# Two attentions on one core: row maxima of four heads in one quad, division by block transposes, interleaved tiles

## The chip, the cores and the metric

One core of a Trainium2 chip runs the whole kernel. The metric is device time in microseconds (us), the median of some runs. The core's engines each work through their own list of instructions in order and meet by semaphores: TensorE (PE in the profile, its weight loads PEld), VectorE (DVE), ScalarE (ACT), GpSimd (POOL), and SyncE (SP), which here only issues DMAs.

## The reference, cut to what matters

A block of two transformer layers over 2048 tokens of width 256. The change touches the two attentions of the second layer, a1 (tokens on themselves, 2048 keys) and a2 (tokens on a context of 1601 keys), both with 16 heads of width 32:

```
q = einsum('bsc,hcd->bhsd', xn, wq); k = einsum('btc,hcd->bhtd', yn, wk); v = einsum('btc,hcd->bhtd', yn, wv)
a = softmax(einsum('bhsd,bhtd->bhst', q, k) * D ** (-0.5), axis=-1)
if causal:
    mask = (arange(t)[None, :] > arange(s)[:, None]).astype(a.dtype)
    a = a * mask
o = einsum('bhst,bhtd->bhsd', a, v)
```

In a1 the mask comes after the softmax and keeps the keys *behind* the query (t > s). So the divisor of a query is a sum over all keys, while the values are summed over the later keys only.

## The kernel before, in words

`attention_stacked` runs once for a1 and once for a2. Four heads form a group (128 = 4 x 32 partitions), and 512 queries a chunk, so there are 4 groups x 4 chunks = 16 chunks, counted by n; n // 4 is the group, n % 4 the chunk in it. Keys go in tiles of 128: 16 in a1, 13 in a2 (the last has 65 rows). A step m is one key tile of one chunk.

*Units ahead of the loop.* q and k are projected in fp32, split by DVE into an f16 high part and an f16 rest (L1240, L1242), and copied by 12 DMAs a unit (L1123) so that 96 partitions hold high, rest and high of one head: one f16 matmul over 96 rows gives a score of nearly fp32 accuracy. `before` lists this lead-in for chunk 0; v units (four key tiles each) stand in it ahead of the first maxima.

*Row maxima.* Every score has to be lowered by its query's maximum before the exponential. For that TensorE computes all scores of chunk n + 1 during chunk n once more (L1338), 512 keys (401 in a2) of one head and 128 queries at a time, into one of three PSUM tiles wb, and DVE reads each with a maximum (L1266): 64 such units a chunk. At its end the 16 x 128 maxima are transposed (L1357), negated on DVE (L1296) and copied by four DMAs into row 96 of qs, so that the score matmul (97 rows) subtracts them.

*A step.* Four score matmuls (L1372, L1369 for passed tiles) go into three PSUM tiles sc in turn; ACT takes the exponential of each into a ring e of weight tiles (3 in a1, 4 in a2). One step later TensorE adds the tile's values into po (L1395, four heads abreast in four column strips) and its weights, against ones, into pd (L1416). Some tiles' weights POOL adds up instead (L1177), and TensorE takes POOL's sum at the chunk's end (L1413). In a1 a tile on the diagonal is first multiplied by a triangle on POOL (L1166). A *passed* tile, one whose keys lie before every query of the chunk, counts in the divisor only: queries go on the partitions and ACT's own sum along the row gives the divisor (L1215). Chunk 0, 1, 2 and 3 of a group have 0, 4, 8 and 12 passed tiles of 16, and all of them come first. `work_at` spreads the units of chunk n + 1 (maxima, projections, division) over the steps, between the matmuls.

*Division.* At a chunk's end ACT copies po and pd out (L1187, L1189). TensorE brings the divisors to 128 x 16 (L1345), DVE adds the passed part and takes reciprocals (L1274, L1276, L1279), TensorE transposes them (L1348), DVE copies (L1282), TensorE spreads them over 128 x 512 (L1354), and DVE multiplies (L1286). After the last chunk the divisions of the last two chunks follow each other.

The order of the work is written out: each engine walks its list, and the places are fixed by `before`, `during`, `work_at` and the loop over m in the code of TensorE.

## Time and profile before

| | |
|---|---|
| median of 3 runs | 3877.21 us (3872.72 to 3889.8) |
| span of the profiled execution, which is its own time | 3882.5 us |
| mean granted clock of TensorE | 0.917 of 2.4 GHz |
| busy in the whole span | PE 87%, DVE 64%, ACT 50%, POOL 37% |
| lead-in and loop of a1 | 70.7 and 918.3 us |
| loop of a2 | 804.4 us |

The page gives no other time for the profiled execution than its span. A share over the whole span mixes stages with other limits; each stage has to be read by itself. A row of a timeline gives start, duration, engine, line, operation, destination <- sources, count, and in brackets the idle time before with what ended it.

### The profile page before, as it was taken

What the parts mean: (1) busy time and instruction counts of PE and PEld (TensorE: products, weight loads), DVE (VectorE), ACT (ScalarE), POOL (GpSimd) and SP (SyncE); (2) the same over time, 40 slices, a digit from 0 to 9 for tenths busy, and PEclk for the clock granted to TensorE, in tenths of its full rate; (3) what the DMA queues carried; (4) which work ended last, traced back from release to release, by engine and by line L of the source; (5) the groups of instructions that cost most, each with busy time, mean ns of one, the idle gap of its engine ahead of it and who ended that gap; (6) DMA issues with size and microseconds to landing.
All of it is one profiled execution on the core that took longest, in us unless ns stands there. A gap on an engine that the chain in (4) does not pass through costs nothing. (4 is left out here: it accounts for less than half of the span.)

```text
span 3882.5 us, 65515 instructions
## 1 busy us (share of the span) xinstructions
PE 3392.2 (87%) x22711; PEld 1574.6 (41%) x22711; DVE 2480.8 (64%) x4757; ACT 1950.3 (50%) x3913; POOL 1423.1 (37%) x719
## 2 busy tenths in 40 slices
PE   5999999725994899999999986899999998969998
PEld 2333333414773233333332264233333232657776
DVE  5877687374114778777787355777777772555665
ACT  2777777421112257566666733255555555423443
POOL 2000000253222241434226140366666666505553
PEclk7999899866997799999999887799999999969999
DMA  1000000177772100100000030100000000437445
GB/s 58 11 15 10 13 6 6 66 271 257 229 241 91 33 13 9 25 6 17 17 9 5 1 107 23 39 14 17 14 15 14 8 9 1 130 112 258 93 83 116
DMA packets 163212, 239.02 MB, mean 62 GB/s; under 512 B 35859, under 2 KB 132826, under 8 KB 155994
## 3 DMA queue, kind: packets, MB, share of 16 engines
q1 hardware_dynamic: 142698, 209.40, 16.9%
q0 software_dynamic: 19056, 24.88, 3.5%
q8 instruction: 176, 2.88, 0.3%
q14 instruction: 130, 1.06, 0.1%
q10 hardware_dynamic: 1152, 0.79, 0.1%
HBM read 136.44 MB, written 68.92 MB: 53 GB/s over the span
## 5 line engine op out<-in xcount | busy, mean ns | idle before, releaser
L1266 DVE TENSOR_REDUCE a_part_max<-a_wb 128x1 f32<-128x512 f32 (+1 forms) x2048 | 1162.0, 625 | 232.3 <-PE a_wb L1338 221.7
L1218 ACT ACTIVATE a_e<-a_sc 128x512 f32<-128x512 f32 (+1 forms) x1472 | 795.2, 599 | 693.2 <-PE a_sc L1372 686.3
L1177 POOL TENSOR_TENSOR a_part_sum<-a_part_sum,a_e 128x2048 f32<-128x2048 f32 x160 | 724.6, 4528 | 103.3 <-ACT a_e L1218 87.1
L1338 PE MATMUL a_wb<-a_ks,a_qs 96*128 96x512 f16 (+1 forms) x2048 | 738.9, 372 | 26.5 <-DVEq L1246 9.5
L1372 PE MATMUL a_sc<-a_qs,a_ks 97*128 97x512 f16 (+1 forms) x1472 | 545.7, 384 | 11.7 <-DMA a_qs<-a_neg_max 8.1
L757 DVE TENSOR_REDUCE xa_part_max<-xa_mx 128x2 f32<-128x802 f32 x512 | 471.4, 986 | 128.1 <-PE xa_mx L864 125.4
L693 ACT ACTIVATE xa_e<-xa_sc 128x512 f32<-128x512 f32 (+1 forms) x832 | 445.6, 597 | 130.2 <-PE xa_sc L851 122.7
L1338 PEld LDWEIGHTS a_wb<-a_ks,a_qs 96*128 96x128 f16 x2048 | 200.6, 98 | 620.6 <-DVE a_part_max L1266 451.6
L1395 PE MATMUL a_po<-a_e,a_v 128*32 128x512 f32 (+1 forms) x2432 | 324.0, 605 | 1.9 <-ACT a_dc L1189 1.0
L1166 POOL TENSOR_TENSOR a_em<-a_e,a_later 128x512 f32<-128x512 f32 x64 | 80.9, 1265 | 579.1 <-issue 365.8
L887 PE MATMUL xa_po<-xa_e,xa_v 128*32 128x256 f32 (+1 forms) x3328 | 269.5, 396 | 7.5 <-ACT xa_oc L743 2.6
L1215 ACT ACTIVATE a_e<-a_sc 128x512 f32<-128x512 f32 x384 | 223.4, 646 | 29.4 <-PE a_sc L1369 28.5
L1372 PEld LDWEIGHTS a_sc<-a_qs,a_ks 97*128 97x128 f16 (+1 forms) x1472 | 145.5, 100 | 175.3 <-ACT a_e L1218 65.2
L864 PE MATMUL xa_mx<-xa_khi,xa_qhi 32*128 32x401 f16 x1024 | 180.1, 351 | 19.7 <-DVE xa_part_max L757 15.3
L1416 PE MATMUL a_pd<-a_e,ones 128*32 128x512 f32 (+1 forms) x1440 | 193.0, 608 | 0.0
L2607 POOL DMA_INDIRECT routed_sums<-moe_ye,moe_ids x79 | 140.1, 1773 | 141.2 <-DVE moe_ye L2750 136.7
L851 PE MATMUL xa_sc<-xa_qs,xa_ks 49*128 49x512 f16 (+1 forms) x832 | 176.7, 393 | 12.6 <-DMA xa_qs<-xa_neg_max 12.6
L2646 PE MATMUL moe_g<-wall,moe_xt 128*128 (+1 forms) x666 | 171.5, 315 | 1.0 <-ACT moe_xt L2698 0.8
L2646 PE MATMUL moe_up<-wall,moe_xt 128*128 (+1 forms) x666 | 169.8, 314 | 0.0
L635 POOL CAST xa_qhi<-xa_raw 128x512 f16<-128x512 f32 x16 | 9.8, 610 | 429.4 <-ACT xa_raw L705 421.7
L1369 PE MATMUL a_sc<-a_ks,a_qs 97*128 97x512 f16 x384 | 149.1, 407 | 8.8 <-ACT a_e L1215 7.1
L1175 POOL COPY a_part_sum<-a_e 128x2048 f32<-128x2048 f32 x28 | 52.9, 1890 | 278.2 <-ACT a_e L1218 270.7
(362 smaller groups left out, 4589.5 us busy)
## 6 DMA issues: line engine op xcount, KB each, us to landing
experts_w_up<-in_we SPq DMA_DIRECT2D x32, 1024.0 KB, 6.5
wall<-expert_halves SPq DMA_DIRECT2D x18, 1088.0 KB, 7.1
experts_w_down<-in_we SPq DMA_DIRECT2D x32, 512.0 KB, 6.0
a_qs<-a_stage SPq DMA_DIRECT2D x360, 32.0 KB, 1.9
moe_xr<-sorted_rows SPq DMA_DIRECT2D x79, 136.5 KB, 2.1
a_ks<-a_stage SPq DMA_DIRECT2D x336, 32.0 KB, 1.9
choose_whole<-in_wm SPq DMA_DIRECT2D x18, 544.0 KB, 9.0
expert_halves<-choose_cut SPq DMA_DIRECT2D x18, 544.0 KB, 8.3
```

The source lines that it names most:

```text
L693: act.activation(e[:r, m % ering, j, :], src[:r, :], ACT.Exp, scale=scale).then_inc(s_taken, 1)
L757: dve.tensor_reduce(part_max[:, 2 * h:2 * h + 2, t, c], src[:, :, :mxw], AX.X, ALU.max).then_inc(m_taken, 1)
L887: last = pe.matmul(po[h:h + SLOT, q], w, e[:r, m % ering, j, q], start=(kt == first and part == 0), stop=stop)
L1177: pool.tensor_tensor(part_sum[:, :, :], part_sum[:, :, :], tile, ALU.add).then_inc(pool_added, 1)
L1215: act.activation(e[:, m % ering, j, :], sc[(HG * m + j) % NSC][:, :], ACT.Exp, scale=scale, accum_out=span_sum[:, n % 2, t, j, c:c + 1]).t ...
L1218: act.activation(e[:r, m % ering, j, :], sc[(HG * m + j) % NSC][:r, :], ACT.Exp, scale=scale).then_inc(exp_done, 1)
L1266: dve.tensor_reduce(part_max[:, j, t, k:k + 1], src[:, :mxw], AX.X, ALU.max).then_inc(unit_taken, 1)
L1338: last = pe.matmul(dst[:, :mxw], qs[:STACK, j, n % NQ, P * t:P * t + P], ks[:STACK, g % 2, j, mxs[k]:mxs[k] + mxw], start=True, stop=True)
L1372: pe.matmul(sc[i % NSC][:r, :], ks[:STACK + 1, n // NCH % 2, j, P * kt:P * kt + r], qs[:STACK + 1, j, n % NQ, :], start=True, stop=True).t ...
L1395: last = pe.matmul(po[h:h + SLOT, :], w, e[:r, m % ering, j, :], start=(kt == first), stop=stop)
L1416: last = pe.matmul(pd[h:h + SLOT, :], ones[:r, :SLOT], e[:r, m % ering, j, :], start=(kt == first), stop=(kt == nkt - 1))
L2646: last = pe.matmul(dst[:, :], xt[j % 2][:, px, k, :], weights(u, pw, off + EI * k, EI), start=(k == 0 and px == 0 and pw == 0), stop=(k == ...
```

## The change

`attention_stacked` is replaced by `attention_quad`, for both attentions.

- Maxima come from the high halves alone (32 rows). The copies are laid out so that the high part of head j lies on partitions 32j, so the four heads' matmuls stand in four row strips of TensorE: a *quad* is four matmuls (128 queries, 512 keys, four heads) into one tile mx of four PSUM banks, and DVE reads it with two maxima of 2 x 512. There are 16 quads a chunk in a1 and 13 in a2 (the last is of 65 keys). mx is not doubled: the first two heads of a quad wait for DVE's first read of the quad before, the other two for its second.
- Projections, scores, transposition of the maxima and the carried divisors share two PSUM tiles sc (scores alone had three). ACT copies k and q to `raw` (one tile) and POOL splits them; ACT copies v and negates the maxima.
- Division: ACT copies po to ot and pd to dc; DVE transposes dc in blocks of 32 x 32, adds the carried divisors of the passed tiles, takes reciprocals, transposes them back, spread over a block, and multiplies. The passed part reaches the right partitions by a small matmul (carry). TensorE's three steps are gone.
- Passed and kept tiles alternate in the order of the steps. POOL adds other tiles: every other one (5 of 13 in a2 where it had 8). Values of a tile that POOL adds go in two halves of 256 columns.
- In the lead-in the v units stand behind the quads of the second span; POOL fills blanks and ones once all splits of the lead-in are done.

```diff
-def attention_stacked(nc, a, name, wqs, wks, wvs, extra, xq, nkq, xk, nkk, nkeys, scale, causal, ot, ones, bq=None, bk=None, bv=None, ering=4, ones_at=None):
+def attention_quad(nc, a, name, wqs, wks, wvs, extra, xq, nkq, xk, nkk, nkeys, scale, causal, ot, ones, ering=4):
...
-    NWB = 3 if ones_at is None else 4
-    NSC = 3
-    LEAD = 2
...
+    NST, NQ, NR, NSC = 3, 3, 1, 2
+    LEAD = 4
+    home = [(0, 1, 2), (1, 0, 2), (2, 0, 1), (3, 1, 2)]
+    bias_row = [STACK, STACK, STACK, 0]
...
-    def maxima(n, spans=range(nmx)):
-        return [("max", n, t, j, i) for i in spans for t in range(TPC) for j in range(HG)]
...
-        return own_sum and 0 < i and kt < nkt - 2 and (i >= TPC and i % 4 != 3 if causal else kt % 4 != 0)
+        if not causal:
+            return kt % 2 == 1
+        return i >= TPC and i % 4 != 3 if n % NCH == 0 else i % 2 == 1
...
+        tiles += sorted(((n, kt) for kt in range(nkt)),
+                        key=lambda x: (2 * x[1] + 1) * kept if x[1] < skipped else (2 * (x[1] - skipped) + 2) * skipped)
+    def quads(n, spans=range(nspan)):
+        return [("max", n, i) for i in range(nquad) if min(i // TPC, nspan - 1) in spans]
...
+    order = [("k", 0, 0), ("q", 0), ("k", 0, 1)]
+    for c in range(nspan):
+        order += quads(0, [c]) + ([("k", 0, c + 2)] if c + 2 < nspan else [])
+        if c == 1:
+            order += [("v", 0, b) for b in range(nvb)] + [("q", 1)]
+    order += [("rowmax", 0), ("turn", 0)]
...
+        parts = 1 if weighed or not kept or diagonal_of(last_n, last_k) is not None else 2
+        maxima = wide.get(m, [])
+        order += scores[:2] + maxima[:1]
+        order += [("pv", last_n, last_k, 0, parts)] if kept else []
+        order += scores[2:] + lone.get(m, [])
+        order += [("pv", last_n, last_k, 1, parts)] if parts == 2 else []
+        order += [("sum", last_n, last_k)] if weighed else []
+        order += maxima[1:]
+        if maxima and maxima[-1][2] == nquad - 1:
+            order.append(("rowmax", maxima[-1][1]))
...
-        wb = [ps(f"wb{i}", [P, CH]) for i in range(NWB)]
+        mx = ps("mx", [P, HG, CH])
...
+                    pool.tensor_copy(stage[:, i % NST, 0, :w], raw[:, i % NR, :w]).then_inc(high_ready, 1)
+                    pool.wait_ge(high_ready, i + 1)
+                    pool.tensor_tensor(stage[:, i % NST, 1, :w], raw[:, i % NR, :w], stage[:, i % NST, 0, :w],
+                                       ALU.subtract).then_inc(split_ready, 1)
...
+                    act.activation(raw[:, i % NR, :w], src[:, :w], ACT.Copy).then_inc(s_taken, 1)
...
-                    dve.tensor_reduce(part_max[:, j, t, k:k + 1], src[:, :mxw], AX.X, ALU.max).then_inc(unit_taken, 1)
...
+                    dve.wait_ge(m_ready, quad_at[u] + 1)
+                    for h in range(0, HG, 2):
+                        if i < TPC * nfull:
+                            dst, src = part_max[:, h:h + 2, i % TPC, i // TPC], mx[:, h:h + 2, :]
+                        else:
+                            dst = part_max[:, h:h + 2, :, nfull]
+                            src = mx[:, h:h + 2, :TPC * tail].rearrange("p j (t k) -> p j t k", t=TPC)
+                        dve.tensor_reduce(dst, src, AX.X, ALU.max).then_inc(m_taken, 1)
...
+                    dve.transpose(tr[:, :], dc[:, :]).then_inc(norm_step, 1)
+                    dve.reciprocal(inverse[:, :], den).then_inc(norm_step, 1)
+                    dve.transpose(dc[:, :].rearrange("p (b r) -> p b r", r=SLOT), over(inverse[:, :], SLOT)).then_inc(norm_step, 1)
+                    dve.tensor_tensor(ot[:, g, o:o + CH], ot[:, g, o:o + CH], dc[:, :], ALU.mult).then_inc(divided, 1)
...
-                    last = pe.matmul(dst[:, :mxw], qs[:STACK, j, n % NQ, P * t:P * t + P],
-                                     ks[:STACK, g % 2, j, mxs[k]:mxs[k] + mxw], start=True, stop=True)
...
-                    pick = a["ident"][:, :].rearrange("p (j d) -> p j d", d=SLOT)[:, :, den_at]
-                    for t in range(TPC):
-                        last = pe.matmul(dst[:, HG * t:HG * t + HG], dc[:, P * t:P * t + P], pick, start=True, stop=True)
-                    last = pe.transpose(dst[:HG * TPC, :P], inverse[:, :, :].rearrange("p t j -> p (t j)"), a["ident"][:, :])
-                        last = pe.matmul(dst[:, P * t:P * t + P], pick_head[:, P * t:P * t + P], inverse_t[:, :], start=True, stop=True)
...
+                        if m and j % 2 == 0:
+                            pe.wait_ge(m_taken, 2 * m - 1 + j // 2)
+                        rows = slice(SLOT * j, SLOT * j + SLOT)
+                        if i < TPC * nfull:
+                            o, w, dst = CH * (i // TPC), CH, mx[:, j, :]
+                        else:
+                            o, w, dst = CH * nfull, tail, mx[:, j, tail * t:tail * t + tail]
+                        last = pe.matmul(dst, qs[rows, j, n % NQ, P * t:P * t + P], ks[rows, g % 2, j, o:o + w], start=True, stop=True)
...
-                        attention_stacked(nc, a, p, ws["q"], ws["k"], ws["v"],
-                                          [(wo[:, :, :], a[p + "_wo"])], xq, KC, xk, nkk, nkeys, SLOT ** -0.5, n == 0,
-                                  ot, ones, ering=3 if n == 0 else 4)
+                        attention_quad(nc, a, p, ws["q"], ws["k"], ws["v"], [(wo[:, :, :], a[p + "_wo"])], xq, KC, xk, nkk, nkeys, SLOT ** -0.5, n == 0,
+                                       ot, ones, ering=3 if n == 0 else 4)
```

The first place is TensorE in the lead-in of a1; the names are those of the tiles, wb, mx and sc in PSUM. Before:

```order
L1314 MATMUL a_wb<-a_xk,a_wk 128x512 x2
L1318 MATMUL a_wb<-a_xq,a_wq 128x512 x2
L1314 MATMUL a_wb<-a_xk,a_wk 128x512 x2
L1325 MATMUL a_wb<-a_wv,a_xk 128x128 x32
L1338 MATMUL a_wb<-a_ks,a_qs 128x512 x16
L1314 MATMUL a_wb<-a_xk,a_wk 128x512 x2
L1338 MATMUL a_wb<-a_ks,a_qs 128x512 x16
L1314 MATMUL a_wb<-a_xk,a_wk 128x512 x2
L1318 MATMUL a_wb<-a_xq,a_wq 128x512 x2
L1338 MATMUL a_wb<-a_ks,a_qs 128x512 x32
L1357 MATMUL a_wb<-ident,a_row_max 16x128
L1372 MATMUL a_sc<-a_qs,a_ks 128x512
```

After:

```order
L1367 MATMUL a_sc<-a_xk,a_wk 128x512 x2
L1371 MATMUL a_sc<-a_xq,a_wq 128x512 x2
L1367 MATMUL a_sc<-a_xk,a_wk 128x512 x2
L1414 MATMUL a_mx<-a_ks,a_qs 128x512 x16
L1367 MATMUL a_sc<-a_xk,a_wk 128x512 x2
L1414 MATMUL a_mx<-a_ks,a_qs 128x512 x16
L1367 MATMUL a_sc<-a_xk,a_wk 128x512 x2
L1378 MATMUL a_sc<-a_wv,a_xk 128x128 x32
L1371 MATMUL a_sc<-a_xq,a_wq 128x512 x2
L1414 MATMUL a_mx<-a_ks,a_qs 128x512 x32
L1478 MATMUL a_sc<-ident,a_row_max 16x128
L1394 MATMUL a_sc<-a_qs,a_ks 128x512 x2
```

The v units (L1325, L1378) moved from ahead of the first maxima to a place between those of the second and the third span, and the maxima (L1338) became as many matmuls of the quads (L1414).

The second place is TensorE in the loop of a2, one step with values and weights. Before:

```order
L1395 MATMUL a_po<-a_e,a_v 32x512 x4
L1338 MATMUL a_wb<-a_ks,a_qs 128x401
L1372 MATMUL a_sc<-a_qs,a_ks 128x512
L1338 MATMUL a_wb<-a_ks,a_qs 128x401 x2
L1372 MATMUL a_sc<-a_qs,a_ks 128x512
L1338 MATMUL a_wb<-a_ks,a_qs 128x401
L1416 MATMUL a_pd<-a_e,ones 32x512 x4
L1338 MATMUL a_wb<-a_ks,a_qs 128x401
L1372 MATMUL a_sc<-a_qs,a_ks 128x512
L1338 MATMUL a_wb<-a_ks,a_qs 128x401
L1372 MATMUL a_sc<-a_qs,a_ks 128x512
L1338 MATMUL a_wb<-a_ks,a_qs 128x401
```

After, the same step and the one behind it, whose weights POOL adds:

```order
L1414 MATMUL a_mx<-a_ks,a_qs 128x512 x4
L1436 MATMUL a_po<-a_e,a_v 32x512 x4
L1394 MATMUL a_sc<-a_qs,a_ks 128x512 x2
L1459 MATMUL a_pd<-a_e,ones 32x512 x4
L1394 MATMUL a_sc<-a_qs,a_ks 128x512 x2
L1414 MATMUL a_mx<-a_ks,a_qs 128x512 x4
L1436 MATMUL a_po<-a_e,a_v 32x256 x4
L1394 MATMUL a_sc<-a_qs,a_ks 128x512 x2
L1436 MATMUL a_po<-a_e,a_v 32x256 x4
```

Single maxima stood between all other matmuls; now one quad stands behind the second score of a step, and the values of the second tile come in two halves.

The third place is DVE in a chunk of a1 with passed tiles, around the division. Before:

```order
L1266 TENSOR_REDUCE a_part_max<-a_wb 128x1 x7
L1274 TENSOR_REDUCE a_total<-a_span_sum 128x16
L1276 TENSOR_TENSOR a_total<-a_total,a_wb 128x16
L1279 RECIPROCAL a_inverse<-a_total 128x16
L1266 TENSOR_REDUCE a_part_max<-a_wb 128x1 x4
L1282 COPY a_inverse_t<-a_wb 16x128
L1266 TENSOR_REDUCE a_part_max<-a_wb 128x1 x4
L1286 TENSOR_TENSOR a_ot<-a_oc,a_wb 128x512
L1266 TENSOR_REDUCE a_part_max<-a_wb 128x1 x37
```

After:

```order
L1313 TENSOR_REDUCE a_part_max<-a_mx 128x2 x10
L1329 TENSOR_REDUCE a_total<-a_span_sum 128x16
L1334 TENSOR_TENSOR a_by_block<-a_total,a_in_block 128x64
L1313 TENSOR_REDUCE a_part_max<-a_mx 128x2 x8
L1341 STREAM_TRANSPOSE a_tr<-a_dc 128x512
L1347 TENSOR_TENSOR a_divisor<-a_tr,a_carried 128x16
L1351 RECIPROCAL a_inverse<-a_divisor 128x16
L1354 STREAM_TRANSPOSE a_dc<-a_inverse 128x512
L1358 TENSOR_TENSOR a_ot<-a_ot,a_dc 128x512
```

The reciprocal, the copy and the product stood apart, with maxima between them; now a chain of five instructions stands in one piece.

## Rows read from the trace of the kernel before

**Rows 1.** The head of the profile page.

```profile
span 3882.5 us, 65515 instructions
```

**Rows 2.** Windows view: busy of PE, PEld, DVE, ACT, POOL, then PEclk, DMA, GB/s.

```profile
1245.00:1315.70 70.70, 58.30 (x153) 20.41 (x154) 50.09 (x82) 1.28 (x1) 15.96 (x6) 0.67 0.16 42
1315.70:2234.00 918.30, 873.27 (x5089) 288.28 (x5093) 671.52 (x1116) 590.96 (x1438) 320.99 (x124) 0.98 0.05 12
1557.00:1620.50 63.50, 62.04 (x383) 19.80 (x382) 46.85 (x77) 35.73 (x70) 38.67 (x12) 1.00 0.10 25
1620.50:1685.90 65.40, 62.10 (x399) 24.67 (x398) 46.15 (x75) 36.94 (x83) 25.05 (x9) 1.00 0.04 11
1685.90:1741.60 55.70, 53.12 (x300) 17.27 (x299) 46.44 (x78) 38.20 (x99) 11.48 (x6) 0.97 0.03 8
1741.60:1791.70 50.10, 47.33 (x242) 15.68 (x242) 41.99 (x72) 37.94 (x110) 5.06 (x4) 1.00 0.06 13
2482.00:3286.40 804.40, 778.39 (x4636) 244.39 (x4634) 552.54 (x1096) 461.73 (x862) 537.42 (x128) 0.99 0.05 13
```

**Rows 3.** Timeline of PE, one step in the loop of a1 (start us, us).

```profile
1659.52 1.07 PE L1395 MATMUL a_po<-a_e,a_v 128*32 128x512 f32 x8
1660.51 0.39 PE L1338 MATMUL a_wb<-a_ks,a_qs 96*128 96x512 f16 x1
...
1661.71 1.07 PE L1416 MATMUL a_pd<-a_e,ones 128*32 128x512 f32 x8
...
1663.68 1.07 PE L1395 MATMUL a_po<-a_e,a_v 128*32 128x512 f32 x8
```

**Rows 4.** Timeline of PE in the first attention.

```profile
302.78 0.64 PE L887 MATMUL xa_po<-xa_e,xa_v 128*32 128x256 f32 x8
303.35 0.34 PE L864 MATMUL xa_mx<-xa_khi,xa_qhi 32*128 32x401 f16 x2
303.63 0.39 PE L851 MATMUL xa_sc<-xa_qs,xa_ks 49*128 49x512 f16 x2
```

**Rows 5.** Timeline of DVE in two lead-ins, first attention and a1.

```profile
37.69 7.30 DVE L757 TENSOR_REDUCE xa_part_max<-xa_mx 128x2 f32<-128x802 f32 x8 [1.27 <-PE xa_mx L864]
...
1262.47 9.66 DVE L1266 TENSOR_REDUCE a_part_max<-a_wb 128x1 f32<-128x512 f32 x16 [1.50 <-PE a_wb L1338]
```

**Rows 6.** Timeline of PE in the lead-in of a1.

```profile
1262.06 0.81 PE L1338 MATMUL a_wb<-a_ks,a_qs 96*128 96x512 f16 x3 [1.81 <-issue]
1263.22 0.39 PE L1338 MATMUL a_wb<-a_ks,a_qs 96*128 96x512 f16 x1 [0.35 <-DVE a_part_max L1266]
```

**Rows 7.** Groups by line on PE, loop of a1 (busy, mean ns | idle before).

```profile
L1354 PE MATMUL a_wb<-a_inverse_t,a_pick_head 16*128 16x128 f32 x112 | 16.2, 283 | 0.0
L1345 PE MATMUL a_wb<-ident,a_dc 128*128 128x4 f32 x115 | 14.9, 252 | 0.5 <-DVE a_part_max L1266 0.5
...
L1357 PE MATMUL a_wb<-ident,a_row_max 128*16 128x128 f32 x15 | 4.0, 270 | 14.5 <-DVE a_row_max L1291 14.5
```

**Rows 8.** Groups by line on POOL, loops of the first attention and of a1.

```profile
L637 POOL TENSOR_TENSOR xa_low<-xa_raw,xa_qhi 128x512 f16<-128x512 f32 x14 | 16.2, 1159 | 1.1
L635 POOL CAST xa_qhi<-xa_raw 128x512 f16<-128x512 f32 x14 | 8.5, 610 | 421.7 <-ACT xa_raw L705 421.7
...
L1177 POOL TENSOR_TENSOR a_part_sum<-a_part_sum,a_e 128x2048 f32<-128x2048 f32 x48 | 217.4, 4528 | 35.6 <-ACT a_e L1218 31.0
```

**Rows 9.** Timeline of POOL and PE at the start of a1.

```profile
1245.20 13.75 POOL L1137 MEMSET a_ks<- 1x16384 f16 x1 [50.68 <-POOLq L223]
...
1254.83 5.41 PE L1325 MATMUL a_wb<-a_wv,a_xk 128*128 128x128 f32 x47
```

**Rows 10.** Timeline of PE, ACT and DVE at the end of a2.

```profile
3286.31 1.87 PE L1345 MATMUL a_wb<-ident,a_dc 128*128 128x4 f32 x8
...
3292.32 0.60 ACT L1187 ACTIVATE a_oc<-a_po 128x512 f32<-128x512 f32 x1 [14.21 <-DVE a_ot L1286]
...
3298.74 0.69 DVE L1286 TENSOR_TENSOR a_ot<-a_oc,a_wb 128x512 f32<-128x512 f32 x1 [2.22 <-PE a_wb L1354]
```

More of the change, by code:

```diff
@@ new lines, in attention_quad @@
+    if not causal:
+        tiles = [(n, kt) for n in range(NC) for kt in range(nkt)]
+    place_of = {tile: m for m, tile in enumerate(tiles)}
+    def quads(n, spans=range(nspan)):
[5 more added lines that the diff above has]
+            order += [("v", 0, b) for b in range(nvb)] + [("q", 1)]
@@ new lines, in attention_quad @@
+    for m in range(nkt * NC + 1):
+        n, kt = tiles[m] if m < nkt * NC else (NC, 0)
+        last_n, last_k = tiles[m - 1]
+        scores = [("s", n, kt, j) for j in range(HG)] if n < NC else []
+        kept = m and not passed(last_n, last_k)
+        weighed = kept and not on_pool(last_n, last_k)
+        parts = 1 if weighed or not kept or diagonal_of(last_n, last_k) is not None else 2
[8 more added lines that the diff above has]
+            order.append(("rowmax", maxima[-1][1]))
+        if 0 < n and m == nkt * n:
+            order.append(("out", n - 1))
```

605 lines of the change are left out of this document (310 added, 295 removed).

## Prediction

> **What bounds the kernel now.** I read the profile's head for the time [rows 1], then the windows view stage by stage [rows 2]. The change touches two stages: a1, the causal attention with 16 key tiles, and a2, with 13 key tiles. Each has a lead-in (first maxima, about 70 us) and a loop of 16 chunks. The loops take 918.3 and 804.4 us, and TensorE is busy 95% and 97% of them at a granted clock of 0.98 and 0.99 (2.4 GHz nearly throughout), DVE 73% and 69%, ACT 64% and 57% [rows 2]. So TensorE's order is the bound, except where a chunk has many passed tiles. The four chunks of one head group in a1 (0, 4, 8 and 12 passed tiles of 16) take 63.5, 65.4, 55.7 and 50.1 us [rows 2].
>
> A step on TensorE is one key tile: four scores, some maxima, values (L1395), weights (L1416). From the start of L1395 to the next one is 4.16 us (1659.52 to 1663.68), with five maxima in it; the values hold 1.0 us (1659.52 to 1660.51), the five f16 matmuls after them 1.20 (to 1661.71), 0.22 each and 0.1 of switching, and the weights with four f16 slots 1.97 [rows 3]. So 0.88 scores + 1.0 + 1.0 + 1.1 maxima + 0.18 of switching = 4.16.
>
> **Price of a quad on TensorE.** No row shows four heads abreast. The first attention runs two abreast: a pair of 401 columns holds 0.28 us (303.35 to 303.63) [rows 4]. Below, four in one slot: 0.28 plus 111 more columns at 0.22/512 us = 0.33. Above, two pair slots one after the other: 0.65. I take 0.40, near the lower end, as rows 4 show two fully side by side. The Trainium skill, page "TensorE: Matmul & The Clock Gate", section "Measured speedup vs the span model", gives 3.07 times for four row groups; by it the quad is 4 x 0.22 / 3.07 = 0.29, an estimate, and the sum below would be 464 x 0.11 = 51 us lower.
>
> **Price of a quad on DVE.** Maxima of 512 columns take 9.66/16 = 0.604 us, pairs of 401 (802 elements) 7.30/8 = 0.912 [rows 5], so 1.06 ns for each element and 1.15 us for 1024. A quad has two: 2.30. Its only tile mx is refilled in between: DVE's first maximum ends at 1262.47 + 0.60 = 1263.07, the matmul it frees starts at 1263.22 (0.15), and a matmul begun at 1262.06 is read at 1262.47 (0.41) [rows 5, 6]. The second half of a quad waits for the last read of the one before, and the next read waits for that half: 2.30 + 0.56 = 2.86 us a quad. Bounds: 2.30 if nothing is exposed, 3.07 at half clock, where 512 columns take 0.21 more.
>
> **Steps after.** With weights: 4.16 - 1.1 + 0.40 = 3.46 us. In a1 a step had four maxima (64 over 16), so 3.94 before; in a2 4.9 of 401 columns at about 0.18, so 3.95. A kept tile that POOL adds: 3.94 - 1.0 = 2.94 before; after, 3.46 - 2.0 + 2 x 0.57 for values in two halves (302.78 to 303.35 [rows 4]) = 2.60, which DVE's cycle lifts to 2.86. A passed tile: before, 4 x 0.604 = 2.42 (DVE's maxima; TensorE needs 8 x 0.22 = 1.76); after, TensorE needs 0.88 + 0.40 = 1.28, but a quad still goes with each, so 2.86. This is the price of the change: passed steps get 0.44 longer.
>
> **Division.** Per chunk TensorE loses L1345 and L1354, (14.9 + 16.2)/14 = 2.2 us [rows 7], and one small transposition: 2.5. On DVE two block transposes come in. No row has one; the nearest is the 512-element product, 0.69 us [rows 10], so I take 0.69 each (bounds 0.55, one element a cycle by rows 5, and 1.4). Two of them replace a copy, about +1.3 us of DVE a chunk. Behind them in DVE's queue waits the next quad's read, and TensorE waits at the quad after it: hidden where steps are 3.46 (0.6 to spare each), 2.5 us in chunks of mostly passed tiles. The transposition of the row maxima costs TensorE (4.0 + 14.5)/15 = 1.2 us a chunk, nearly all of it waiting for DVE [rows 7]; now the row maxima are issued a step earlier: 0.5.
>
> **What is costed at nothing.** ACT takes over the copies of k, q and v and the negated maxima, some 3 us a chunk: 38 of 50 us become 41 [rows 2], hidden by TensorE's steps; uncovered it is 0.7 a copy. The splits on POOL (1.77 each) are a chunk early; only POOL's adds wait behind them (below).
>
> **Chunk by chunk, a1** (counts of tiles from the code; q and k units of two fp32 matmuls, 0.88 each as the values are; v 7.4 by rows 9; 1.0 for POOL's sum). Before: 8 x 3.94 + 8 x 2.94 + 5.3 + 1 + 2.5 + 1.2 = 65.0 against 63.5 measured; the four by the same prices 65.0, 62.0, 62.8, 50.2 = 240, measured 234.7, so the prices are 2% high. After: 8 x 3.46 + 8 x 2.86 + 5.3 + 1 + 0.5 = 57.4, and 1.5 because POOL's adds (4.53 us each [rows 8], three in four steps, now with the splits between them) hold back the ring of three weight tiles: 58.9. Second: 7 x 3.46 + 9 x 2.86 + 6.8 = 56.8. Third: 5 x 3.46 + 11 x 2.86 + 10.7, less 4 of q and v that fit into the slack of passed steps, plus 2.5 for division = 58.0. Fourth: 4 x 3.46 + 12 x 2.86 + 0.7 + 2.5 = 51.4. Sum 225, so -15 a group; -11 in the last, which has no k and v to hide. **Loop of a1: -56 us.** Interleaving passed and kept tiles gives only these 4 us: ACT needs about 38 us of a 50 us chunk [rows 2], so passed steps are paced by DVE, and a step has no buffer to lend its slack to the next.
>
> **a2.** Before 5 x 3.95 + 8 x 2.95 + 1 + 3.2 + 2.5 + 1.2 = 51.2, measured 804.4/16 = 50.3. After, POOL adds 5 tiles where it added 8: 8 x 3.46 + 5 x 2.86 + 1 + 3.2 + 0.5 = 46.7. Loop: 16 x 4.5 = **-72 us.** DVE needs 13 x 2.86 + 3 = 40 there, so it doesn't bind.
>
> **Lead-ins.** Nothing hides here. a1: 16 quads x 2.86 = 45.8 for 64 x 0.604 = 38.7: +7. The v units, done before while the first DMAs landed, now stand between the quads of the second and third span: 47 of 64 took 5.41 us [rows 9], +7.4 for all. One raw tile goes through ACT and POOL (0.61 + 1.16 [rows 8], where DVE did two 0.69 steps), q behind k: +2. Together +16. POOL's blanks, 22016 elements at 13.75/16384 us [rows 9] = 18.5, lie beside the last eight quads (23 us). a2: 12 quads and a short one 36.5 for 64 x 0.486 = 31: +5; v +3; raw +2; its blanks, 14.7 us, start later against fewer reads: +1. Together **+27 us.** SP's list keeps its 12 copies a unit, so no queue gets longer.
>
> **Ends.** After the last weights two divisions ran one behind the other, 3286.31 to 3299.43 = 13.1 us [rows 10]. After: two copies 1.2, two transposes 1.4, the small steps 0.5, the product 0.7, handoffs 0.6: 4.4. Twice: **-17 us.**
>
> **Sum.** -56 - 72 + 27 - 17 = -118; +5 for stretches at half clock in passed-heavy chunks: -113. Against the profiled execution's 3882.5 [rows 1]: 3769; the median of the runs, 3877.2, lies 5 below it: 3764. I say 3765.
>
> **Rivals.**
> *Both loops better than priced.* A quad holds 0.33 and short steps run at 2.60 where DVE gets ahead: 464 x 0.07 + 32 x 5 x 0.26 = 74 us more: 3690. For it: rows 4. Against: the single mx tile. Chance 0.17.
> *No gain: the rings are too short.* mx is one tile where three wb rotated, and scores, projections and v share two sc banks where scores had three. If TensorE comes to a bank 0.24 us late in each of 464 steps, 113 us are gone: 3877. For it: restart and matmul latency (0.56) equal one exponential (38 us over 64, about 0.57), so two banks are just enough and no more. Against: between the second score and the third stand quad and values (1.4 us), so their banks are free by then. The Trainium skill, page "Perfetto Trace Analysis", section "Matmuls", asks that independent groups rotate through PSUM banks so that evacuation overlaps; by that rule this rival is what happens. Chance 0.13.
> *Slower: the clock.* A passed step leaves TensorE idle 1.6 of 2.86 us. In the lead-in of a1, also paced by DVE, the granted clock is 0.67, in the fourth chunk, with TensorE busy 94%, 1.00 [rows 2]. If chunks three and four fell to 1.2 GHz, their 48 kept steps would take some 3 us more: +144, so 3909. It decides above about 80% of those steps; kept tiles now stand between passed ones, which speaks against it. Chance 0.09.
> *My sum*, 3765, own range 3720 to 3815: chance 0.61.
>
> **How the numbers follow.** Within 0.5% (19 us) is about what a measurement of this kernel can't tell from no change. Faster by over 0.5% (below 3858): the sum, the better case and a sixth of the short rings: 0.80. Within: 0.09. Slower: the clock and a worse ring: 0.11. The range from 3690 to 3860 leaves out about 0.08 below, half of the better case, and 0.12 above.
>
> **What would show it.** Mean chunk in a1 near 55 us with the fourth no shorter than before; in a2 near 45.8. Matmuls of mx in fours within 0.45 us; DVE's 128x1024 maximum at 1.15 us and about 0.56 us idle between quads where tiles are passed. Lead-ins 86 and 71 us. The prediction fails if score matmuls wait for ACT in kept steps, if mx is waited for in steps with weights, or if the clock is below 0.9 in the third and fourth chunks.

## The result: slower by 1.8%

The changed kernel takes 3951.0 us (median of 4 runs, 3944.7 to 3955.1); the kernel before, beside it, 3879.1. The ratio is 1.018, its 95% interval 1.016 to 1.021. The forecast was 3765, and 3951 lies above its range and above the times of all three rivals.

The windows view of the kernel after, for the stages of [rows 2] (columns: stretch, length, busy time and instructions of PE, PEld, DVE, ACT, POOL, then the granted clock, DMA share, GB/s): a1's lead-in and loop, chunks 2 to 4 of its second group and chunk 1 of its third, a2's lead-in and loop.

```profile
1246.50:1330.40 83.90, 40.94 (x154) 17.08 (x155) 38.29 (x34) 7.52 (x12) 30.10 (x21) 0.64 0.14 35
1330.40:2337.70 1007.30, 870.96 (x5291) 243.79 (x5294) 622.82 (x590) 628.26 (x1503) 385.48 (x180) 0.87 0.05 11
1662.10:1727.00 64.90, 54.84 (x353) 14.42 (x349) 44.25 (x39) 39.25 (x92) 29.01 (x14) 0.95 0.08 19
1727.00:1795.70 68.70, 58.71 (x357) 22.22 (x349) 40.70 (x40) 41.77 (x107) 17.66 (x9) 0.90 0.03 7
1795.70:1856.90 61.20, 53.79 (x241) 12.95 (x233) 40.71 (x40) 40.04 (x115) 8.08 (x7) 0.69 0.03 7
1856.90:1919.10 62.20, 56.55 (x433) 15.56 (x433) 41.50 (x38) 37.61 (x73) 44.43 (x18) 0.97 0.08 20
2516.50:2584.40 67.90, 28.94 (x108) 11.22 (x109) 29.81 (x27) 6.71 (x12) 24.23 (x16) 0.58 0.16 38
2584.40:3361.10 776.70, 732.58 (x5409) 179.59 (x5413) 480.07 (x465) 488.71 (x916) 361.91 (x132) 0.98 0.06 13
```

The loop of a1 is 89 us longer than in [rows 2], not 56 shorter; that of a2 is 28 shorter, not 72. The lead-ins, 83.9 and 67.9, are near the forecast 86 and 71. In a1 PE is busy for 86% of the loop where it was 95, DVE 62 for 73, ACT 62 for 64; only POOL rises, from 35 to 38%. PE's clock falls from 0.98 to 0.87. Time went into waiting, and then into running slowly after the wait.

**The prices of single operations held, but for the quad.** PE's timeline in chunk 2 (start, length, operation, count, in brackets idle time before and its releaser):

```profile
1693.28 0.39 PE L1414 MATMUL a_mx<-a_ks,a_qs 32*128 32x512 f16 x4
1693.61 1.06 PE L1436 MATMUL a_po<-a_e,a_v 128*32 128x512 f32 x8
...
1696.68 0.40 PE L1414 MATMUL a_mx<-a_ks,a_qs 32*128 32x512 f16 x4
...
1699.46 0.46 PE L1414 MATMUL a_mx<-a_ks,a_qs 32*128 32x512 f16 x4
```

The prediction priced an operation from its start to the start of the next one. So a step with weights takes 3.40 us (1693.28 to 1696.68; taken: 3.46), and a step that POOL adds 2.78 (2.86). A quad holds 0.33 (1693.28 to 1693.61), not the 0.40 taken: its row is 0.39 long, but the next matmul starts earlier. This is the lower bound that the prediction named, all four heads in one slot. By the prediction's count of 464 quads the sum was 32 us too high here, so its miss elsewhere was larger by that.

**Where a1 lost.** DVE's timeline in a first chunk, where the division stands between two quads' maxima:

```profile
1614.72 0.70 DVE L1341 STREAM_TRANSPOSE a_tr<-a_dc 128x512 f32<-128x512 f32 x1
1615.45 1.39 DVE L1347 TENSOR_TENSOR a_divisor<-a_tr,a_carried 128x16 f32<-128x16 f32 x1
1616.87 0.25 DVE L1351 RECIPROCAL a_inverse<-a_divisor 128x16 f32<-128x16 f32 x1
1617.16 0.71 DVE L1354 STREAM_TRANSPOSE a_dc<-a_inverse 128x512 f32<-128x512 f32 x1
1617.91 0.69 DVE L1358 TENSOR_TENSOR a_ot<-a_ot,a_dc 128x512 f32<-128x512 f32 x1
```

PE's timeline from shortly before, and the windows view of the last stretch:

```profile
1608.55 1.98 PE L1367 MATMUL a_sc<-a_xk,a_wk 128*128 128x512 f32 x4 [0.47 <-ACT a_e L1247]
...
1619.79 0.39 PE L1414 MATMUL a_mx<-a_ks,a_qs 32*128 32x512 f16 x2 [1.52 <-DVE a_part_max L1313]
1620.92 0.61 PE L1414 MATMUL a_mx<-a_ks,a_qs 32*128 32x512 f16 x2 [0.74 <-DVE a_part_max L1313]
...
1623.77 3.76 PE L1367 MATMUL a_sc<-a_xk,a_wk 128*128 128x512 f32 x4 [0.26 <-ACT a_e L1247]
```
```profile
1622.50:1627.50 5.00, 4.74 (x14) 1.32 (x13) 1.43 (x2) 1.09 (x2) 3.69 (x2) 0.51 0.00 0
```

DVE is away for 3.9 us, PE stands idle 1.52 and 0.74 us, and from the second half of that quad on its matmuls have the length of half clock (1.2 of 2.4 GHz): the window 1622.5 to 1627.5 has a granted clock of 0.51. The k projection in it takes 3.76 us; the one 15 us earlier, at full clock, took 1.98. A wait is paid once as idle time and again in the slower work behind it. In a second chunk the product alone lasts 4.53 us (last section), the division 6.3, and PE stands still for 2.91 us:

```profile
1685.53 0.60 PE L1414 MATMUL a_mx<-a_ks,a_qs 32*128 32x512 f16 x2 [2.91 <-DVE a_part_max L1313]
```

The second place is a diagonal tile, here in the timeline of the last chunk, all engines:

```profile
2319.74 1.26 POOL L1204 TENSOR_TENSOR a_em<-a_e,a_later 128x512 f32<-128x512 f32 x1 [12.77 <-ACT a_e L1247]
...
2321.15 1.11 PE L1440 MATMUL a_po<-a_e,a_v 128*32 128x256 f32 x8 [0.82 <-ACT a_e L1244]
...
2322.61 1.03 PE L1391 MATMUL a_sc<-a_ks,a_qs 97*128 97x512 f16 x2
...
2323.26 0.60 ACT L1244 ACTIVATE a_e<-a_sc 128x512 f32<-128x512 f32 x1 [2.21 <-PE a_sc L1391]
```

POOL masks the tile until 2321.00, and PE begins the tile's values 0.15 us later, after 0.82 us of idle time. (The row names ACT, whose exponentials ended at the same moment; the values wait for the mask.) Scores 2 and 3 of the next tile are queued behind the values. So ACT is idle for 2.21 us: 0.1 until the values start, 1.46 for the values, which here run at half clock, and 0.65 until the first score is ready.

### The profile page after: what moved, and what is told of

Its sections match the earlier page's. It is cut to its first block and busy times, and to the rows that moved or that the text cites. A ratio compares the mean times of both kernels' runs of the same rounds, so it can differ in the third digit from the quotient of the medians.

```text
span 3951.9 us, 66931 instructions
## 1 busy us (share of the span) xinstructions
PE 3299.8 (83%) x23639; PEld 1443.4 (37%) x23639; DVE 2335.7 (59%) x3490; ACT 2026.4 (51%) x4053; POOL 1337.2 (34%) x806
## 3 DMA queue, kind: packets, MB, share of 16 engines
q14 instruction: 127, 1.04, 0.1%
## 5 line engine op out<-in xcount | busy, mean ns | idle before, releaser
L1313 DVE TENSOR_REDUCE a_part_max<-a_mx 128x2 f32<-128x1024 f32 (+1 forms) x928 | 1076.6, 1202 | 649.0 <-PE a_mx L1414 649.0
L1218 POOL TENSOR_TENSOR a_part_sum<-a_part_sum,a_e 128x2048 f32<-128x2048 f32 x116 | 526.8, 4541 | 280.9 <-ACT a_e L1247 278.6
L1394 PE MATMUL a_sc<-a_qs,a_ks 97*128 97x512 f16 (+1 forms) x1472 | 502.6, 403 | 52.2 <-ACT a_e L1244 11.9
L1436 PE MATMUL a_po<-a_e,a_v 128*32 128x256 f32 (+2 forms) x3456 | 359.2, 488 | 0.0
L1414 PE MATMUL a_mx<-a_ks,a_qs 32*128 32x512 f16 (+1 forms) x2048 | 247.8, 384 | 111.3 <-DVE a_part_max L1313 87.3
L1394 PEld LDWEIGHTS a_sc<-a_qs,a_ks 97*128 97x128 f16 (+1 forms) x1472 | 111.9, 98 | 571.1 <-ACT a_e L1247 397.1
L1459 PE MATMUL a_pd<-a_e,ones 128*32 128x512 f32 (+1 forms) x1792 | 252.7, 637 | 0.0
L1192 POOL CAST a_stage<-a_raw 128x512 f16<-128x512 f32 (+1 forms) x64 | 37.5, 586 | 512.7 <-ACT a_raw L1254 502.1
L1414 PEld LDWEIGHTS a_mx<-a_ks,a_qs 32*128 32x128 f16 x2048 | 64.6, 92 | 319.2 <-DVE a_part_max L1313 149.1
L1391 PE MATMUL a_sc<-a_ks,a_qs 97*128 97x512 f16 (+1 forms) x384 | 153.4, 448 | 28.2 <-ACT a_e L1244 14.3
```

Of the source, the lines that this page charges most:

```text
L1218: pool.tensor_tensor(part_sum[:, :, :], part_sum[:, :, :], tile, ALU.add).then_inc(part_added, 1)
L1313: dve.tensor_reduce(dst, src, AX.X, ALU.max).then_inc(m_taken, 1)
L1394: pe.matmul(dst[:r, :], ks[rows, g % 2, j, P * kt:P * kt + r], qs[rows, j, n % NQ, :], start=True, stop=True).then_inc(s_ready, 1)
L1414: last = pe.matmul(dst, qs[rows, j, n % NQ, P * t:P * t + P], ks[rows, g % 2, j, o:o + w], start=True, stop=True)
L1436: last = pe.matmul(po[h:h + SLOT, lo:hi], w, e[:r, m % ering, j, lo:hi], start=opens, stop=stop)
L1459: last = pe.matmul(pd[h:h + SLOT, :], ones[:r, :SLOT], e[:r, m % ering, j, :], start=(kt == first), stop=(kt == last_kt))
```

## The experiments

The first attention, which no kernel touches, takes 579 to 623 us in these profiles, from the first copy of po to the last (last section). That is as much as most edits are worth, so profiles are compared by loops: the 15 chunks between the first copy of po and the last one in each attention, and the second group's four chunks, from the starts of these copies. Sums over 15 chunks of the same code repeat within 1 us (the old a1 in four profiles 852.7 to 853.4, the new a2 707.6 and 707.7 in four), but the new a1 was profiled only once for each kernel, and chunks with equal work differ by up to 7 us between the groups of one profile. r1, u1, z1 and all1 leave something out, so what they return isn't the block's result. Under each heading stand the windows of a1's 15 chunks and, where it matters, a2's. For the kernel before, a1 alone, and for the changed kernel:

```profile
1386.80:2240.20 853.40, 808.22 (x4722) 270.19 (x4720) 618.60 (x1034) 553.67 (x1366) 282.31 (x112) 0.98 0.05 11
```
```profile
1406.40:2337.60 931.20, 804.47 (x4846) 226.59 (x4842) 573.11 (x547) 588.82 (x1430) 340.38 (x161) 0.87 0.04 11
2653.40:3361.10 707.70, 672.53 (x5056) 165.91 (x5048) 438.48 (x428) 455.91 (x856) 336.71 (x121) 1.00 0.05 13
```

| kernel | time (runs) | first attention | 15 chunks of a1 | chunks 1 to 4 of group 2 | 15 chunks of a2 |
|---|---|---|---|---|---|
| before | 3879.1 (4) | 588.7 | 853.4 | 63.5 65.4 55.7 50.1 | 751.4 |
| prediction | 3765 | | | 58.9 56.8 58.0 51.4 | |
| after | 3951.0 (4) | 579.0 | 931.2 | 63.7 64.9 68.6 61.2 | 707.7 |
| f1, zeros in passed steps | 3965.1 (4) | 623.4 | 930.7 | 63.4 66.1 70.2 56.3 | 707.7 |
| r1, third score bank | 3870.9 (1) | 588.7 | 878.1 | 63.6 60.5 59.5 58.3 | 683.0 |
| u1, no k, v units | 3856.2 (1) | 588.7 | 867.6 | 55.8 57.2 58.7 60.1 | 682.1 |
| z1, no division | 3881.5 (1) | 578.8 | 894.3 | 58.4 58.6 67.4 58.0 | 691.0 |
| m1, diagonal values later | 3913.0 (1) | 578.8 | 902.7 | 62.0 63.7 63.4 60.0 | 707.7 |
| n1, passed tiles first | 3930.9 (1) | 595.4 | 897.9 | 63.8 62.8 66.8 57.0 | 707.6 |
| s1, division in pieces | 3950.7 (1) | 623.4 | 901.9 | 60.1 63.2 67.6 58.2 | 694.4 |
| c1 = m1 + n1 + s1 | 3876.6 (10) | 578.8 | 868.3 | 59.8 60.1 60.1 55.1 | 694.4 |
| all1 = z1 + u1 + m1 + n1 | 3786.0 (1) | 595.5 | 809.4 | 55.3 55.0 54.9 53.8 | 664.8 |

### h1: the old a1 with the new a2

```
+which = attention_stacked if n == 0 else attention_quad
```


> The old attention in a1, the new one in a2. It splits the loss between the two. By the trace of the changed kernel a2 alone gives back: loop 804 to 775, lead-in +8, end -8, so about 29 us less than before: 3848 to 3852. By the prediction's prices (loop -72, lead-in +11, end -8) it would be 70 less: 3808. If the new a2 is slower only because something of the new a1 carries over into it, the loop of a2 falls below 765.

Measured: 3852.3 us, ratio 0.994 (0.991 to 0.998). The new a2 gives 24 us back alone, a third of its forecast; the loss is all in a1. The 15 chunks of a2 take 704.5 here, so the new a1 carries only 3 us over into a2.

### f1: TensorE kept busy in passed steps

```
+busy = n < NC and passed(n, kt) and m % nkt and any(not passed(*t) for t in tiles[nkt * n:m - 1])
+order += [("fill", n, x) for x in range(2 * busy)]     # ahead of and behind scores[2:]
...
+pe.matmul(pd[0:SLOT, :], zero[0:STACK + 1, :], ks[0:STACK + 1, (u[1] // NCH) % 2, 0, 0:CH], start=False, stop=False)
```


> In passed steps TensorE gets four more f16 matmuls of zeros (128 x 512, added to pd, so the result stays the same), from the second kept tile's place on. Clock theory (idle time in passed steps takes TensorE's clock to half, and kept steps then run at half): the granted clock of the fourth chunk rises from 0.69 to above 0.9, the chunk falls from 61 to about 50 us, the loop of a1 from 1007 to about 950. Ring theory (two banks between TensorE and ACT): clock up but chunks as long as before, or longer by the 0.9 us of zeros where TensorE is behind; loop 1000 to 1030.

```profile
1440.90:2371.60 930.70, 817.19 (x5122) 236.91 (x5118) 573.22 (x547) 588.38 (x1430) 340.71 (x161) 0.93 0.04 11
```

The clock rose from 0.87 to 0.93, the 15 chunks stayed at 931. In group 2 the fourth chunk is 4.9 us shorter although 8 of its steps carry 0.88 us more of matmuls (8 x 4 x 0.22 = 7 us); the second and third are 1 to 2 longer. Group 3 does nearly the same, but in group 1 the fourth chunk is 0.8 us and the third 5.7 us longer. So half clock seems to cost something where passed tiles prevail. The 57 us of the clock theory did not come, but the run doesn't refute them: the zeros are 272 matmuls, by 0.22 us each some 60 us of TensorE's time (an estimate), and the loop is no longer for them. What this rise of the clock is worth lies between nothing, if all zeros fit into idle time, and about these 60 us.

### r1: a third bank for scores and units

```
-    NST, NQ, NR, NSC = 3, 3, 1, 2
+    NST, NQ, NR, NSC = 3, 3, 1, 3
...
-        po, pd = ps("po", [P, CH]), ps("pd", [P, CH])
+        po = ps("po", [P, CH])
+        pd = po
```


> Three score banks in place of two. The bank comes from pd: the weights are summed into the bank of the values (same matmuls, but the divisors and values are mixed up, so the output isn't the reference's; the weights of a chunk's first kept tile go before its values). Ring theory: PE's waits for ACT in passed steps and around the projections go, chunks fall to the predicted 59, 57, 58, 51, loop of a1 about 900, loop of a2 745 or less. Clock theory: TensorE still has idle time in passed steps, the fourth chunk stays near 60 us at a clock near 0.7, loop of a1 above 980.

```profile
1404.80:2282.90 878.10, 766.16 (x4846) 222.60 (x4844) 572.81 (x547) 569.90 (x1429) 339.57 (x160) 0.88 0.05 11
2597.10:3280.10 683.00, 659.78 (x5052) 163.00 (x5050) 440.24 (x428) 453.30 (x854) 335.75 (x120) 1.00 0.06 13
```

53 us off a1 and 25 off a2, at the same clock in a1. The short ring is a real part of the loss, 78 of the 113 us that the rival gave it, but not all: chunk 1 does not move. PE's wait for the single mx tile takes its place. In the 15 chunks of a1 it was (us in total, times, longest) for the changed kernel, then for r1:

```profile
PE a_mx L1414 <- DVE a_part_max L1313: 21.9, 29, 2.9
```
```profile
PE a_mx L1418 <- DVE a_part_max L1317: 54.1, 72, 3.5
```

### u1: no projections of k and v after group 0

```
-        if g + 1 < NG:
+        if g + 1 < 1:        # and parity 0 of ks and v for every group
```


> The projections of k and v for head groups 1 to 3 are left out; all groups use the keys and values of group 0 (the output isn't the reference's). Queries are still projected. The prediction priced them at 1.76 a k unit, 7.4 for the four v units, less some hidden: 12 us a group, 37 us over a1. Unit theory (they go through the two score banks and ACT, and each stops the scores): 28 us a group as chunks with and without them differ, 85 us, loop of a1 near 920. Clock theory: the units cost what they cost on TensorE, at half clock in part: 40 to 55 us, loop 955 to 970, with the fourth chunk still 55 to 61 us at a clock of 0.7.

```profile
1403.50:2271.10 867.60, 755.61 (x4614) 187.04 (x4610) 561.10 (x547) 575.90 (x1408) 323.29 (x141) 0.86 0.03 7
```

64 us, between the 37 of the prediction and the 85 of the unit theory. Group 2 costs 27 us more with its units (258.4 against 231.8), group 3 22, where 10.4 to 12 were priced (4 x 1.76 + 7.4, less up to 4 hidden). Without units the first chunk is at its price (55.8; 58.9 less two units is 55.4), but the fourth, which has none, is still 60. So the units are one part, and something else stretches chunks with passed tiles.

### z1 and s1: the division left out, and in three pieces

```
-            put(n, LEAD + 4, ("norm", n - 1))                                  # z1
...
+            for x in range(3):                                                 # s1
+                put(n, LEAD + 4 + 2 * x, ("norm", n - 1, x))
```


> The division is left out in both attentions (the two block transposes, the reciprocal, the sum of divisors and the product on DVE; the output is not the reference's). Division theory: in the middle of each chunk this chain of 2.6 us (6 to 7 where the product runs beside an addition of POOL) keeps DVE from the next quad, TensorE waits 2 to 3 us for it, its clock falls to half and the projections and kept steps behind it run at half. Then each chunk of a1 is 3 to 6 us shorter, the 15 chunks from the first end to the last 931 to about 860, the second chunk of a group most, and TensorE's wait for DVE at the quads goes. The prediction priced the chain at 0 in the first two chunks and 2.5 in the last two. Unit theory: the chain is mostly hidden, 931 to 910 or more.

> The division on DVE is cut into three pieces, two steps apart: transposition, sum and reciprocal; second transposition; product. Division theory: the pieces (1.2, 0.7 and 0.7 us) fit into DVE's 0.6 us of slack a step or nearly, TensorE's waits of 2 to 3 us a chunk become several of 0.1 to 0.6, the clock holds in the first two chunks; 15 chunks of a1 931 to about 885. If the whole DVE time counts and not the length of the stop, 931 stays within 10. a2: 708 to 690 by the one, 708 by the other.

The windows of z1:

```profile
1398.00:2292.30 894.30, 783.59 (x4846) 222.77 (x4842) 523.34 (x476) 588.15 (x1430) 338.95 (x161) 0.89 0.05 11
```

Those of s1, and DVE's timeline in its a2:

```profile
1453.60:2355.50 901.90, 784.99 (x4850) 221.43 (x4842) 570.92 (x547) 587.99 (x1430) 339.87 (x161) 0.89 0.05 11
2666.80:3361.20 694.40, 667.89 (x5056) 165.87 (x5052) 468.60 (x428) 456.01 (x855) 336.74 (x121) 1.00 0.06 13
```
```profile
2744.22 3.01 DVE L1347 TENSOR_TENSOR a_ot<-a_ot,a_dc 128x512 f32<-128x512 f32 x1
```

The division costs 37 us in a1 and 17 in a2. Cut in pieces, with all its work still done, it gives back 29 and 13 of them. So it isn't DVE's time that costs, but the stop that it makes for TensorE: PE's wait for mx falls from 21.9 to 8.3 us in the 15 chunks of a1, and from 8.2 to nothing in those of a2. In s1's a2 DVE is even busy for 30 us more, since 14 of the products last 3.0 us beside an addition of POOL, and the loop is 13 us shorter all the same. There the long piece stands behind the quad of 65 keys, whose reading takes 1.31 us where a full quad's takes 2.36. The 860 expected of z1 did not come. Its gains in group 2 are 5.3 and 6.3 us in the first two chunks, where the division took 3.9 and 6.3, and 1.2 and 3.2 in the others, where it took 2.7; in group 1 the third chunk is even 4 longer.

### m1: values of diagonal tiles behind scores 2 and 3

```
-        order += [("pv", last_n, last_k, 0, parts)] if kept else []
-        order += scores[2:] + lone.get(m, [])
+        values = [("pv", last_n, last_k, 0, parts)] if kept else []
+        masks = kept and diagonal_of(last_n, last_k) is not None
+        order += scores[2:] + lone.get(m, []) + values if masks else values + scores[2:] + lone.get(m, [])
```


> The values of diagonal tiles (four a chunk) go behind the next tile's scores 2 and 3 in TensorE's order, instead of ahead of them. Mask theory: TensorE stands before these values until POOL has masked the tile (1.26 us after the last exponential), and ACT starves since scores 2 and 3 are queued behind; so each of 4 diagonal tiles a chunk costs 1 to 2 us, most in the fourth chunk, where all kept tiles are diagonal: fourth chunk 61 to 55, the 15 chunks of a1 931 to 880. If the mask is not the point (clock, units, division), 931 stays within 10, or gets longer by 0.3 a diagonal tile, since score 2 then comes to its bank before ACT has freed it. a2 has no mask: 708 as before.

```profile
1397.40:2300.10 902.70, 785.10 (x4850) 226.38 (x4842) 573.28 (x547) 588.65 (x1430) 339.56 (x161) 0.89 0.05 11
```

29 us off a1, where 50 were expected; nothing off a2. ACT's wait for passed tiles' scores in the 15 chunks, in the kernel before, the changed kernel and m1:

```profile
ACT a_e L1215 <- PE a_sc L1369: 26.9, 47, 1.1
```
```profile
ACT a_e L1244 <- PE a_sc L1391: 110.9, 99, 3.9
```
```profile
ACT a_e L1245 <- PE a_sc L1392: 81.0, 89, 3.4
```

The wait shrinks by 30 us, which is what the loop gains. The fourth chunk falls by 1 us only, not by 6. PE's own wait for the mask isn't new: in these 15 chunks its values wait for POOL for 12.8 us in the kernel before and 11.4 in the changed one. What m1 takes away is the place of the values ahead of scores that ACT waits for; how much of that is the mask's time and how much the values' own, the run doesn't separate.

### n1 and c1: passed tiles first, and the three edits together

```
-                        key=lambda x: (2 * x[1] + 1) * kept if x[1] < skipped else (2 * (x[1] - skipped) + 2) * skipped)
+                        key=lambda x: x[1])
```


> The passed tiles of a chunk stand first, as in the kernel before, instead of between the kept ones. Clock theory: TensorE has a long stretch with idle time, the whole of it at half clock, but the kept tiles behind it run at full clock: fourth chunk's half-clock time stays near 35 us, but falls on passed tiles, which DVE paces: chunks 3 and 4 get shorter by 3 to 5 us. Mask theory: diagonal tiles stand side by side, and ACT has a kept step of 3.4 us between them, so the wait for POOL stays: no gain. The prediction gave interleaving 4 us a group: without it 931 becomes 947.

> Three edits of their own runs together, in both attentions: passed tiles first, values of diagonal tiles behind scores 2 and 3, the division in three pieces. Alone they took 33, 29 and 29 us off the 15 chunks of a1 (931). If they act on different waits, 840; if passed tiles first and later values mend the same wait for the mask, 865 to 875. a2 has only the division: 694. Time 3846 by the first, 3875 by the second; before 3876.

Windows of n1: its 15 chunks, five passed steps in its fourth chunk, and a stretch of kept steps behind them:

```profile
1420.30:2318.20 897.90, 787.04 (x4850) 224.65 (x4842) 561.40 (x547) 587.78 (x1427) 341.48 (x162) 0.84 0.05 11
1819.40:1834.80 15.40, 13.55 (x40) 2.66 (x40) 11.88 (x12) 12.76 (x43) 0.00 (x0) 0.50 0.01 2
1845.00:1860.00 15.00, 13.37 (x105) 3.81 (x105) 8.83 (x10) 9.20 (x18) 6.32 (x6) 1.00 0.02 5
```

Windows of c1, two stretches with the same instructions, in the third chunks of groups 2 and 3:

```profile
1701.40:1738.00 36.60, 29.94 (x192) 14.81 (x196) 25.66 (x25) 25.78 (x73) 5.60 (x4) 0.95 0.04 11
1938.20:1981.60 43.40, 38.14 (x192) 19.95 (x196) 25.80 (x25) 25.86 (x72) 5.60 (x4) 0.72 0.04 9
```

Interleaving costs 33 us; the prediction had it save 4 us a group. Side by side, a passed step takes 15.4/5 = 3.08 us at a clock of 0.50, which is the bound of 3.07 that the prediction named for half clock, and the kept steps behind run at 1.00. The clock over the whole loop is lower than in the changed kernel (0.84 against 0.87), and the loop is shorter. This fits the clock theory, by which interleaving moves half clock onto the kept steps, but no run sets that apart from the waits. In c1 (3876.6 us, ratio 0.999, 0.995 to 1.002: no change against before) the three edits take 63 us, not the 91 of their sum, so they overlap. The two stretches of c1 have the same work, a clock of 0.95 against 0.72, and differ by 6.8 us: so much goes with the clock where the v units stand in passed steps.

### all1: all of it taken out

The edits of z1, u1, m1 and n1 together.

> Everything that single runs found costly in a1 is taken out together: no division, no projections of k and v for groups 1 to 3 (group 0's are used; neither gives the reference's output), passed tiles first, values of diagonal tiles behind scores 2 and 3. By the prediction's prices without these parts a group is 55.4 + 53.3 + 47.2 + 48.9 = 205 us, the 15 chunks about 768. If the four effects are apart and are the whole loss, the run shows 768 (931 - 37 - 64 - 33 - 29); if two are the same wait, about 795; if something is still unnamed (half clock in passed steps by itself, the two-bank ring), above 810, with the fourth chunk still 55 or more.

```profile
1416.20:2225.60 809.40, 738.11 (x4618) 185.40 (x4610) 528.56 (x476) 577.07 (x1405) 323.25 (x142) 0.82 0.03 7
```

122 us in place of 163, so effects overlap by 41. By the prediction's prices the four chunks are 55.4, 53.3, 50.3 (58.0 less 7.4 of v and 2.5 of division, and 2.2 more since q alone is hidden; the 47.2 of the expectation took 3 too much off) and 48.9; they took 55.3, 55.0, 54.9 and 53.8. What is left, 11 us a group, grows with the passed tiles. 24 passed steps a group at 3.08 instead of 2.86 would be 5 of it, an estimate from the stretch of n1; the other 6 stay open. The clock of this loop, 0.82, is lower than in the changed kernel, and the loop is the shortest: so half clock without the waits goes with only 11 us a group over the prices at full clock (13 with the quad at 0.33 in the 24 steps with weights).

### h3 and h4: the old a1, the new a2 with pieces, then with a shorter lead

```
-    LEAD = 4
+    LEAD = 2        # h4 only
```


> The old attention in a1, the new one in a2 with its division in three pieces. The old a1 with the new a2 took 3852; the pieces took 13 us off the 15 chunks of the new a2: 3839. If the 13 us came from an undisturbed clock that this kernel has already, 3852.

> As the kernel with the old a1 and the new a2 with its division in pieces, but the maxima of a chunk run two steps ahead of it, not four (LEAD 2 in place of 4), so that the first chunk of a2 spreads its 13 quads over 11 steps, not 9. First-chunk theory: the first chunk took 69 us in a2 where the later ones take 46 to 50, since in steps with two quads TensorE waits for DVE (6.9 us of waits) and runs at half clock; then it falls to 60 to 64 and the time from 3850 to about 3843. If the first chunk is long for another reason (the first exponentials, the load of the bias rows), it stays at 69. Later chunks: as before if the bias rows arrive within two steps (7 us), 2 to 4 us longer each if not, and the time 3880 to 3900.

PE's waits for DVE and the window of the first chunk of a2, in h3:

```profile
PE a_mx L1419 <- DVE a_part_max L1314: 6.9, 10, 0.9
```
```profile
2502.00:2568.00 66.00, 57.04 (x360) 13.26 (x363) 41.60 (x37) 32.80 (x61) 25.20 (x11) 0.90 0.08 19
```

The same in h4:

```profile
PE a_mx L1419 <- DVE a_part_max L1314: 2.9, 4, 0.9
```
```profile
2477.00:2536.10 59.10, 53.79 (x352) 12.97 (x355) 36.89 (x33) 32.80 (x62) 25.24 (x11) 0.92 0.09 21
```

h3 took 3850.2 us, ratio 0.992 (0.989 to 0.995), where 3839 was expected: the 15 chunks of a2 are 10 us shorter than in h1 (694.4 against 704.5), but the times of h1 and h3 can't be told apart. h4 took 3839.2, ratio 0.987 (0.983 to 0.990), the best ratio of the kernels that leave nothing out. Crowding two quads into a step of the first chunk cost 7 us (66.0 to 59.1); the later chunks lose 4.6 in sum (694.4 to 699.0). So LEAD explains 2 of the 11 us between the two; their intervals overlap.

## Why the prediction was wrong

**The step that failed** is the chunk-by-chunk sum of a1: the loop became 89 us longer where -56 was forecast, 145 us of the miss of 186. Its prices for single operations held or were too high. What failed is adding steps as if each cost the larger of its engines' work at full clock, with nothing carried over in the queues. By its parts:

- *Division, "hidden where steps are 3.46".* The transposes had their price (0.70 and 0.71 for 0.69). But 0.6 us of slack a step hides a chain only if it is spread over steps; in one piece PE waits, then runs at half clock. And the chain took 3.9 us in first chunks and 6.3 in second ones, where POOL's work held it. z1 gives 37 us in a1 where 2.5 in two chunks a group, 20 in all, were priced, and 17 in a2, where it was costed at nothing.
- *"4 of q and v that fit into the slack of passed steps".* The units cost 64 us where 31 to 37 were priced (u1). So slack of TensorE was not room for them. Likely reasons, which no run sets apart, are that passed steps can run at half clock (0.50 in n1) and that the units pass through the two score banks.
- *"Interleaving passed and kept tiles gives only these 4 us."* It costs 33 (n1). The values of a diagonal tile also stand ahead of scores that ACT waits for, which the sum did not have (m1: 29, partly the same time).
- *"What is costed at nothing", ACT's copies.* ACT is busy for only 62% of the loop, but TensorE also waits for it at the two score banks: with a third bank the 15 chunks are 53 and 25 us shorter (r1), with the same copies on ACT. How much of this is the copies and how much the exponentials, r1 doesn't separate. The rival of short rings was half right. The Trainium skill, page "Perfetto Trace Analysis", section "Matmuls", asks that independent matmul groups rotate through PSUM banks, so that the emptying of one overlaps the next one's matmuls; r1 agrees in direction, three banks 878, two 931.
- *+5 for half clock.* The rival of the clock was right that the fourth chunk falls (0.69). The size was too large: 144 us are 36 a group, and all1, at a clock of 0.82, lies 11 to 13 a group above the prices at full clock. How much the clock adds to the waits of the changed kernel stays open; c1 shows 6.8 us in one stretch, and f1's rise by 0.06 is worth between nothing and some 60.

**a2** gained 28 us, not 72. The division took 17 (z1), the first chunk 14 (68.4 where 58.8 less 4.5 was due), 7 of which are its steps with two quads, which the sum left out (h4). The other 13 us are not assigned: u1 and r1 take 26 and 25 off the 15 chunks, each more than is left. Chunks with k or v units take 48.8 to 51.0, those with q alone 46.6, where 46.7 was forecast as the mean of all.

**Right:** the lead-ins; the direction and nearly the size of the end (4.4 forecast; in a2 the last weights start at 3361.68 and last 1.04, the product starts at 3365.20 and lasts 0.69, so 3.2 us lie between the end of the one and of the other; the copy of po runs beside these weights).

The quad at 0.40 was too dear: the trace has 0.33, that is 4 x 0.22 / 0.33 = 2.7 times faster than four matmuls in turn. The Trainium skill, page "TensorE: Matmul & The Clock Gate", section "Measured speedup vs the span model", gives 3.07 times, by which the prediction estimated 0.29; the trace lies between the two, nearer to the page. Of the three signs that it named for its failure two came, and the third in part: kept scores waited for ACT (63 times, 20 us in all in a1's 15 chunks), mx was waited for in steps with weights (6.9 us in a2's first chunk), and the clock fell to 0.69 in the fourth chunk, though in the third only to 0.90.

**Open:** how the 122 us divide where the edits overlap, what half clock adds to the waits, and 6 us a group that remain in all1. A second mx tile, which would take DVE's restart off each quad, was not tried: mx, sc, po and pd fill as many PSUM banks, eight, as wb, sc, po and pd did before. The ring of three weight tiles was not tried either: ACT waits 12.5 us for POOL's additions in a1's 15 chunks where it waited 3.4.
